# A dead write behind GpSimd's indirect DMAs in a graph-attention and mixture-of-experts kernel

## The reference

```python
def _L0_gnn_ref(x, edge_index, W, att_src, att_dst, bias):
    h = (x @ W).reshape(N, H, C)
    a_src = jnp.einsum('nhc,hc->nh', h, att_src)
    a_dst = jnp.einsum('nhc,hc->nh', h, att_dst)
    e = jax.nn.leaky_relu(a_src[src] + a_dst[dst], 0.2)
    m = jax.ops.segment_max(e, dst, num_segments=N)
    e = jnp.exp(e - m[dst])
    denom = jax.ops.segment_sum(e, dst, num_segments=N)
    msg = h[src] * (e / (denom[dst] + EPS))[:, :, None]
    return jax.ops.segment_sum(msg, dst, num_segments=N).mean(axis=1) + bias
...
x = x + _L0_gnn_ref(_layernorm(x), edge_index, W, att_src, att_dst, bias)
x = x + moe(_layernorm(x))        # gelu experts 256 -> 256 -> 256, top 2 of 8
```

## Time and profile before

| what | value |
|---|---|
| median of 3 runs | 972.01 us (971.95 to 973.24) |
| profiled execution, span | 1111.2 us |
| TensorE busy | 718.4 us (65%) |
| VectorE busy | 659.9 us (59%) |
| GpSimd busy | 615.4 us (55%), 680 instructions |
| of that, gathers (line 774) | 375.7 us, 392 instructions |
| mean granted TensorE clock | 0.812 |

### The profile page before, as it was taken

How to read it: one execution, slowest core, us unless ns; L and a number is a source line. 1 busy time by engine, 2 the same in 40 slices (tenths; PEclk the granted TensorE clock), 3 DMA queues, 4 the chain that set the end, 5 groups by cost and what they waited for, 6 DMA issues and landing times.

```text
span 1111.2 us, 16087 instructions
## 1 busy us (share of the span) xinstructions
PE 718.4 (65%) x3704; PEld 640.2 (58%) x3705; DVE 659.9 (59%) x1859; ACT 389.4 (35%) x884; POOL 615.4 (55%) x680
## 2 busy tenths in 40 slices
PE   5783330026474566455565366769999998669995
PEld 4782320025364456455565365768888887558985
DVE  6682470554456456454556665875687878654663
ACT  6521011016463444332312111101354423547763
POOL 6666767706656666566666665001614422476686
PEclk9999555558776777787786677888999999789998
DMA  9633054417676666565554544333999785357763
GB/s 338 201 87 77 4 144 110 113 45 229 203 232 192 199 216 196 155 191 166 168 161 135 154 130 131 117 147 128 395 331 342 279 313 174 110 136 118 120 100 41
DMA packets 97019, 189.64 MB, mean 171 GB/s; under 512 B 22975, under 2 KB 55090, under 8 KB 96092
## 3 DMA queue, kind: packets, MB, share of 16 engines
q0 software_dynamic: 31680, 70.52, 26.3%
q1 hardware_dynamic: 50704, 76.07, 20.2%
q10 hardware_dynamic: 14544, 42.02, 9.7%
HBM read 124.75 MB, written 64.74 MB: 171 GB/s over the span
## 4 chain that ended last, share of the span: by engine, by line
PE 33%; DVE 27%; issue 14%; another core or an unknown queue 13%; DMA 6%; ACT 3%; ACTq 1%; DVEq 1%; POOLq 1%; POOL 0%; SPq 0%; PEld 0%; PEldq 0%
PE banks L1161 13%; PE banks L1035 12%; DMA out<-ring 4%; PE banks L1201 3%; PE banks L1214 2%; DVE banks L1440 2%; DVE arena L1835 1%; PE banks L952 1%; PE banks L966 1%; DMA ring<-in_x 1%; ACT arena L1303 1%; ACT banks L1307 1%; DVE arena L1765 1%; ACTq L1289 1%
## 5 line engine op out<-in xcount | busy, mean ns | idle before, releaser
L774 POOL DMA_INDIRECT ring<-node_table,idx x392 | 375.7, 958 | 217.8 <-issue 110.8
L1035 PE MATMUL banks<-arena,ring 128*128 128x160 f32 x1568 | 298.7, 356 | 114.6 <-ACT banks L1309 51.6
L1035 PEld LDWEIGHTS banks<-arena,ring 128*128 128x128 f32 x1568 | 277.5, 234 | 135.5 <-issue 134.7
L1303 ACT COPY arena<-banks 128x400 f32<-128x400 f32 x200 | 88.5, 494 | 389.5 <-PE banks L1035 133.2
L1161 PE MATMUL banks<-ring 128*128 128x264 f32 x544 | 123.1, 386 | 0.0
L1161 PEld LDWEIGHTS banks<-ring 128*128 128x128 f32 x544 | 103.0, 190 | 17.4
L1835 DVE TENSOR_TENSOR arena<-hot,banks 128x640 f32<-128x640 f32 x84 | 65.0, 817 | 79.2 <-PE banks L1035 39.4
L887 POOL DMA_INDIRECT out<-ring x56 | 89.4, 1596 | 32.3 <-DVE ring L2129 12.3
L1201 PE MATMUL banks<-ring 128*128 128x128 f32 x448 | 65.0, 291 | 16.1 <-issue 14.7
L1201 PEld LDWEIGHTS banks<-ring 128*128 128x128 f32 x448 | 60.9, 203 | 24.6 <-issue 17.6
L1214 PE MATMUL banks<-arena,ring 128*128 x224 | 61.8, 400 | 6.4 <-ACT ring L1357 5.8
(11 more groups left out here) (437 smaller groups left out, 1153.5 us busy)
## 6 DMA issues: line engine op xcount, KB each, us to landing
agg_table<-arena ACTq DMA_DIRECT2D x100, 400.0 KB
ring<-agg_table SPq DMA_DIRECT2D x25, 1600.0 KB
ring<-slot_table SPq DMA_DIRECT2D x56, 130.0 KB
ring<-node_table,idx POOLq DMA_INDIRECT x392
ring<-in_x SPq DMA_DIRECT2D x8, 640.0 KB, 10.9
ring<-in_L_gnn_W SPq DMA_DIRECT2D x4, 1024.0 KB, 7.4
arena<-in_L_ffn_w SPq DMA_DIRECT2D x16, 256.0 KB
node_table<-ring SPq DMA_DIRECT2D x5, 640.0 KB
```

Source lines behind the costliest of these rows:

```text
L774: pool.indirect_dma_start(rows[:, slot_of(b), :], None, node_table, bass.IndirectOffsetOnAxis(idx[:, b:b + 1], 0)).then_inc(got[got_of(g)] ...
L1035: m = pe.matmul(columns[:, k, bass.ds(at * (UNIT * H), SPREAD * H)], lhs[:, k * P:(k + 1) * P], weights, start=False, stop=True, skip_grou ...
L1303: act.copy(stage[j][:, k * SLOTS * H:(k + 1) * SLOTS * H], views[k]).then_inc(drained, 1)
```

## The change

A helper `pause` is added on GpSimd. It writes zeros over `job_i`, which nobody reads any more, raising `pool_chain`; ahead of the write it waits for the count that the last such write (or linked instruction) reached. It is called behind each look-up, behind each gather in `gather`, which serves all groups, and behind each scatter of target scores: 25 + 392 + 25 = 442 writes.

```diff
+            def pause(times=1):
+
+                for _ in range(times):
+                    pool.wait_ge(pool_chain, count[0])
+                    count[0] += 1
+                    pool.memset(job_i[:, :], 0).then_inc(pool_chain, 1)
+
...
                 for t in range(t0, t1):
                     pool.indirect_dma_start(node_block[:, t, :], None, block_rows,
                                             bass.IndirectOffsetOnAxis(block_of_i[:, t:t + 1], 0)).then_inc(node_block_in, 16)
+                    pause()
...
                     pool.indirect_dma_start(rows[:, slot_of(b), :], None, node_table,
                                             bass.IndirectOffsetOnAxis(idx[:, b:b + 1], 0)).then_inc(got[got_of(g)], 16)
+                    pause()
...
                 pool.indirect_dma_start(starts_table, bass.IndirectOffsetOnAxis(starts_at[:, t:t + 1], 0),
                                         score_all[:, t, H:2 * H], None).then_inc(starts_sent, 16)
+                pause()
```

## The result

| | median us | lowest to highest | runs |
|---|---|---|---|
| before | 971.98 | 971.71 to 973.24 | 4 |
| after | 982.29 | 981.27 to 983.80 | 4 |

The changed kernel is slower by 10.3 us: ratio 1.0103, 95% interval 1.0090 to 1.0116. The forecast was 994 us, slower by 22. The sign is right, the size is more than twice too large.

A forecast was written before the change was run, and what follows sets the result against it. GpSimd's issue of indirect DMAs was taken to bound a timed run; 417 scatters and gathers x 0.07 = 29.2 us, less 7 us of room, is 22: 972.0 + 22 = 994 us, range 945 to 1050.

The forecast's parts named there:

- that is my value for what a dead write adds to each DMA: 0.07 us: GpSimd's indirect DMAs: each is 0.07 us longer behind a write; 417 x 0.07 = 29.2 us on GpSimd's chain.
- three rows behind it: Instruction behind a DMA starts at once; plain DMA behind copies has no gap; indirect DMA behind another instruction takes longer.
- I take 7: GpSimd's room in a timed run: 142 - 139 = 3, up to 13 us, taken as 7 and subtracted from the cost.
- I take these standstills as a property of the profiled execution: Engines' idle stretches, nearly all ahead of 725 us: 139 us over the median, taken out of the other engines' time.
- GpSimd is never caught: During the other engines' standstills, GpSimd's 0.30 us gaps between indirect DMAs were said to go on throughout.
- a span that falls while the timed run stays: Sign: changed profile's span falling by tens of us, timed run unchanged, would show standstills belong to the profile, thinned by writes.
- the time grows by 417 times the growth: Sign for scatters and gathers: if time grows by 417 times the period's growth, GpSimd's room was nil.
- I expect 1111 to 1115: Profiled execution of the changed kernel: the edit costs almost nothing there, 1111 to 1115 us, give or take the standstills.
- The lower one, -0.13: Lower bound per DMA: the gap vanishes, period 1.12, the write saves 0.13 us; the faster rival, 27 in 100, 945 us.
- The upper one, 0.23: Upper bound per DMA: the 0.28 us begins only when the write is over, period 1.48, adding 0.23 us.
- that rival: In-line rival, 12 in 100: the write stands fully in line on GpSimd, 417 x 0.23 = 96 less 7, 1061 us.
- Look-ups hidden: The 25 look-ups' writes: 25 x 0.07 = 1.8 us, hidden in the 6.9 us wait ahead of the first gather.

The follow-up runs named there:

- e1: The kernel before, nothing edited, run once more for a second profile: 971.43 us in a calm set, its profiled execution spanning 971.2 us.
- e2: Changed kernel with each dead write one column instead of 56: 973.83 us, ratio 1.0012 to the kernel before, calm set.
- e3: Changed kernel with two 56-column writes behind each DMA, the second waiting for the first: 1079.25 us, ratio 1.1099 to the kernel before, calm set.
- e12: Changed kernel with two writes (56 and 100 columns) behind each DMA that don't wait for each other: 1097.94 us, ratio 0.9800, disturbed set.
- e4: Changed kernel with writes behind the 392 gathers alone, none behind look-ups and scatters: 983.12 us, ratio 1.0115 to the kernel before, calm set.
- e14: Kernel before with 148 gathers of groups 2 to 8 left out, no writes: 919.72 us, ratio 0.9454, calm set.

## Why the prediction was wrong

**The step that failed is the price: "that is my value for what a dead write adds to each DMA: 0.07 us".** Measured: 0.022 (period 1.274 against 1.251 to 1.253), of which 0.017 is the distance between two DMAs, 0.322 against 0.305, and the rest the gather's own length, 0.952 against 0.946 to 0.949. Of the three rows behind it, two led the right way: the write does start at once, and it does lie in the gap. The third was misread. The earlier trace rows have a DMA of 1.04 and 1.01 us behind another kind of instruction, and I put the 0.04 to 0.09 us to that instruction. But each of these is also the first DMA of its batch, and the earlier trace rows had the same: the first scatter takes 1.02, a later one 0.97, with another instruction ahead of neither. The profile after has 1.03, 0.98, 0.97 with a write ahead of each, and its gathers take 0.95. So the instruction ahead is not what lengthens them. What does isn't shown: the first gather of all takes 0.94 in e1, though it too opens a batch. What a write of 0.16 us does cost is that the next DMA starts 0.16 us behind its end: 0.16 + 0.16 = 0.32 against the 0.305 that were there anyway.

**The sum, remade.** Six groups wait for GpSimd, the last of them group 6. Up to its last gather stand 336 gathers and 25 scatters: 361 x 0.022 = 7.9 us. To this come the 1.2 us at four group boundaries, together 9.1; 10.3 were measured. In the two profiles group 6's reader comes 7.7 us later, counted from the first gather (524.1 - 54.2 against 517.2 - 55.0), and the executions themselves are 8.4 us apart, so some 1 us is left that the rows don't place. The prediction had two errors of opposite sign, a price too high and a room too large: with the right price its own count of 417 and its room of 7 us would have given 2 us, no difference. That the sign came out right is luck as far as that goes.

**The room, "I take 7": it is nil.** It was worked out as 142 - 139 from a disturbed execution and a calm median. The difference of two large numbers of two different kinds came out close to the truth, 3 to 13 against 0, by luck, for what it stood on, "I take these standstills as a property of the profiled execution", fell: whole sets of timed runs have them (1117 us), and a profiled execution can be without them (971.2). It also stood on "GpSimd is never caught", which holds for the stretch read there, but not for the whole: the earlier trace rows has 30.6 us of "remote" ahead of the gathers, standstills of GpSimd's own that the sum counts as room. And the sign given for this, a span that falls while the timed run stays, misleads: it fell to 979.6, but e1's fell as far with no write at all. What held is that they are to be taken out of the other engines' time and not out of GpSimd's, and with it the conclusion that GpSimd's row bounds a calm run. The face of the profile, a lead of 20 us, said the opposite. The test "the time grows by 417 times the growth" came out near enough: 417 x 0.022 = 9.2 of 10.3 us.

**"I expect 1111 to 1115" for the profiled execution**: 979.6, since it was a calm one. In the disturbed set, where that sentence belongs, the change doesn't cost 0 to 4 us but gains 13.

**The bounds.** The lower one, -0.13, would have needed the gap to vanish; it doesn't, for a DMA behind a DMA keeps its 0.305 however short the instruction between them (e2). The upper one, 0.23, took 0.28 us from the write's end to the next DMA; 0.16 were measured. The second write of e3 costs 0.19, so beyond the point where the gap is full a write is paid in line, as that rival has it, at a lower price. Where the prediction argues from the gap, the write of 0.17 us "fits inside the gap and adds nothing"; it doesn't ask how long after the write the next DMA can start, and with that the change sits 0.017 us past what is free.

**The rule of dispatch.** The Trainium skill's GPSIMD Engine Reference, section 2.1 (Instruction dispatch), has a core begin the next instruction when its share of the last is done. The writes behind a DMA start at once and the second write of e12 starts 0.08 us behind the first one's start, which agrees; but the next indirect DMA doesn't follow it: it comes 0.15 to 0.165 us behind the last write wherever the write ends late enough. The 71 us that the prediction had for a write on top of the whole gap didn't come.

**Look-ups hidden**: right at this price (e4, 983.12 against 982.29), but the 6.9 us that were to hide them come from a disturbed execution; in e1 the first gather waits 1.4 us, and in e3 the look-ups' writes show.

## What to carry to other kernels

Before an edit is priced from a profile whose execution is far from the median, look for waits on "remote": none stood in the calm executions, and up to 222 us on one engine stood in the disturbed ones, in which VectorE hardly waits for GpSimd's gathers and the sign of this edit's effect turned. A small GpSimd instruction between two indirect DMAs was all but free where it ended 0.11 us behind the first DMA, and cost 0.022 us where it ended at 0.16; from there on all that it was longer was paid, times the number of DMAs, as long as GpSimd's row was the bound. And where a DMA behind a foreign instruction is longer, look for one that is longer without it before the difference is used as a price.

## What the runs showed that was not expected

- The same kernel takes 972 us in one set of runs and 1117 in another, 15% more, by the record on the same chip; most runs of a set lie within 0.3% of its median in the first kind and within 1% in the second.
- In the disturbed sets 442 dead writes make the kernel 1.2% faster, and 884 overlapping ones 2%.
- Two GpSimd writes that don't wait for each other overlap: 0.16 and 0.20 us long, the last ends 0.28 us behind the DMA.
- With half of the gathers of groups 2 to 8 the kernel takes 919.7 us in a calm set, so halving the gathers there is worth some 53 us; e14 leaves out their data too, so it doesn't tell the issue from the transfer.
